# First maxima in four copies over four row groups, and a new order in the opening and the last steps

## The reference

```python
def _mlstm_head(q, k, v, ig, fg):              # per head, 8 heads of 64 channels
    log_fg = jax.nn.log_sigmoid(fg)
    cs = concatenate([0, cumsum(log_fg)])
    log_D = where(ltr, (cs - cs.T)[1:, 1:], -inf) + ig.T
    max_log_D = max(log_D, axis=-1)
    D = exp(log_D - max_log_D)
    C = (q @ (k.T / sqrt(DH))) * D
    normalizer = maximum(abs(C.sum(-1)), exp(-max_log_D))
    return C / (normalizer + EPS) @ v
...
def bitlinear(x, w):                            # x to 8 bit per token, w to -1, 0, 1 times mean(|w|)
    return act_quant(x) @ weight_quant(w).T
g = bitlinear(x, w_gate); u = bitlinear(x, w_up)
h = jnp.square(jax.nn.relu(g)) * u
return bitlinear(h, w_down)
...
x = x + tanh(g_xattn[0]) * attention(_layernorm(x), ctx, ctx, ...)   # heads then divided by their RMS
x = x + tanh(g_ffn[0]) * ffn(_layernorm(x), w_gate, w_up, w_down)
```

## Time and profile before

| | us |
|---|---|
| median of 3 runs | 612.44 |
| the profiled execution's own time | 614.58 |
| its span, first to last instruction | 612.9 |
| TensorE busy | 569.6 (93%) |
| VectorE busy | 526.9 (86%) |
| ScalarE busy | 452.7 (74%) |
| GpSimd busy | 125.9 (21%) |

### The profile page before, as it was taken

The page is one execution under the profiler, slowest core; times in us unless marked ns, Lnnn a source line. Parts: engine busy times, 40 slices in busy tenths (PEclk is TensorE's granted clock), DMA queues, the critical chain, the costliest instruction groups (busy, mean ns, idle before and its releaser), DMA issues.

```text
span 612.9 us, 18356 instructions
## 1 busy us (share of the span) xinstructions
PE 569.6 (93%) x6526; PEld 342.2 (56%) x6605; DVE 526.9 (86%) x1148; ACT 452.7 (74%) x923; POOL 125.9 (21%) x281
## 2 busy tenths in 40 slices
PE   7967578999999999999999999999999999999896
PEld 4744343656556565656556565656565565656443
DVE  4497989898989999898989899898989899897964
ACT  5578868868686868778687868778686968687662
POOL 2236151112121203012121212022121212021100
PEclk9589869999999999999999999999999999999999
DMA  8937305050230506050321405050412305030000
GB/s 319 383 132 250 130 2 190 3 182 28 94 115 18 189 0 206 0 189 17 134 72 39 167 17 189 0 194 13 164 42 76 130 18 190 2 105 1 22 33 34
DMA packets 44113, 62.68 MB, mean 102 GB/s; under 512 B 1848, under 2 KB 25648, under 8 KB 44080
## 3 DMA queue, kind: packets, MB, share of 16 engines
q1 hardware_dynamic: 44080, 62.24, 28.9%
HBM read 53.72 MB, written 8.51 MB: 102 GB/s over the span
## 4 chain that ended last, share of the span: by engine, by line
PE 80%; DVE 10%; issue 5%; ACT 2%; POOL 2%; DMA 1%; SPq 0%; DVEq 0%; ACTq 0%; POOLq 0%
PE yb L1181 17%; PE gb L1155 16%; PE ub L1155 16%; PE tp L1202 8%; PE ab L1189 7%; PE ab L1169 4%; PE tp L1229 3%; PE ab L1212 2%; PE ab L1190 2%; POOL stage L439 1%; PE ab L1263 1%; DVE asum L763 1%; DVE stage L785 1%; DVE dmat L898 1%; DVE stage L770 1%
## 5 line engine op out<-in xcount | busy, mean ns | idle before, releaser
L1155 PE MATMUL ub<-wuT,xqT 128*128 128x512 bf16 x498 | 129.4, 381 | 2.5 <-DVE stage L785 1.7
L1155 PE MATMUL gb<-wgT,xqT 128*128 128x512 bf16 x479 | 127.1, 382 | 4.9 <-issue 4.1
L1181 PE MATMUL yb<-wdT,stage 128*128 128x512 bf16 x482 | 114.3, 379 | 6.6 <-ACT stage L549 3.5
L535 ACT ACTIVATE relu<-gb 128x512 f32<-128x512 f32 x128 | 75.4, 589 | 48.8 <-PE gb L1155 48.4
L785 DVE TENSOR_TENSOR stage<-relu,ub 128x512 f32<-128x512 f32 x128 | 86.8, 678 | 15.9 <-ACT relu L537 15.9
L898 DVE SCALAR_TENSOR_TENSOR dmat<-ab,dmat 128x384 f32<-128x384 f32 x128 | 65.1, 549 | 25.8 <-POOL dmat L447 16.2
L1155 PEld LDWEIGHTS ub<-wuT,xqT 128*128 128x128 bf16 x512 | 49.6, 98 | 64.3 <-DVE stage L785 5.0
L537 ACT ACTIVATE relu<-relu 128x512 f32<-128x512 f32 x128 | 80.8, 631 | 4.1
L1181 PEld LDWEIGHTS yb<-wdT,stage 128*128 128x128 bf16 x512 | 47.0, 98 | 51.7 <-issue 4.3
L1155 PEld LDWEIGHTS gb<-wgT,xqT 128*128 128x128 bf16 x512 | 46.1, 101 | 45.4 <-issue 1.3
L447 POOL TENSOR_SCALAR_AFFINE_SELECT dmat<-dmat 128x256 f32<-128x256 f32 x128 | 55.6, 463 | 66.1 <-ACT dmat L595 50.6
(11 more groups left out here) (124 smaller groups left out, 886.6 us busy)
## 6 DMA issues: line engine op xcount, KB each, us to landing
dmat<-max_rows SPq DMA_DIRECT2D x15, 1024.0 KB, 5.0
values<-in_ctx_v SPq DMA_DIRECT2D x16, 520.0 KB, 7.6
xs<-in_x SPq DMA_DIRECT2D x16, 512.0 KB, 5.8
cT<-in_ctx_t SPq DMA_DIRECT2D x16, 512.0 KB, 6.8
out<-stage SPq DMA_DIRECT2D x32, 256.0 KB, 2.0
stage<-in_w_gate SPq DMA_DIRECT2D x4, 1024.0 KB, 12.2
stage<-in_w_up SPq DMA_DIRECT2D x4, 1024.0 KB, 13.1
stage<-in_w_down SPq DMA_DIRECT2D x4, 1024.0 KB, 5.4
```

The costliest lines, as they stand in the source:

```text
L535: nc.scalar.activation(relu[:, c % 2, :], gb[c % 2][:, :], ACT.Relu).then_inc(g_free, 1)
L1155: last = nc.tensor.matmul(bank[c % 2][:, :], xqT[par][:, t, d, :], w[:, d, c * CH:(c + 1) * CH], start=(d == 0), stop=(d == KD - 1))
L1181: done = nc.tensor.matmul(yb[:, :], hqT[:, c, :], wdT[:, c, :], start=(c == 0), stop=(c == KF - 1))
```

## The change

The scan of batch 0 runs on 128 partitions: a = ig - cs is written into four groups of 32 columns (8 used), so that its transpose has the 8 rows at partitions 0, 32, 64 and 96. `spread_first_max` then takes a different group of rows for each pair of heads. `pick` has ones in row (GROUP + 2) p + e of each group. The numbers of products of ones change, the total of the first weights comes after the next query transposes, and the total of the third weights after the gate products of step 0. Signs and roundings of weights are moved between engines and places. In the last two steps the copies and transposes of hidden values stand earlier.

```diff
-        pick = hq[0][0:NH, :].bitcast(F32)
+        pick = hq[0][:, 0:2 * 2 * P].bitcast(F32).rearrange("p (r c) -> p r c", r=2)
+        GROUP = P // NP
+        a_groups = sb("a_groups", [P, T, NP, GROUP], F32)
...
+            for g in range(NP):
+                if g > 0:
+                    gp.wait_ge(pick_step, g)
+                nc.gpsimd.affine_select(out=pick[:, :, :], in_=pick[:, :, :], compare_op=ALU.not_equal, fill=1.0,
+                                        base=-(GROUP + 2) * g, pattern=[[-1, 2], [0, P]], channel_multiplier=1).then_inc(pick_step, 1)
...  ScalarE, opening
             heads(0, 0)
-            exp_minus_max(0, 0)
             magnitudes(0, 2, 1)
-            for p in range(1, NP):
-                heads(0, p)
+            heads(0, 1)
+            exp_minus_max(0, 0)
+            heads(0, 2)
+            heads(0, 3)
...
-            sign_weight(0, 0)
             forget_gate(1)
             head_rms(0)
             magnitudes(1, 2, 3)
             magnitudes(1, 3, 4)
+            sign_weight(0, 0)
             tokens_rstd(0)
-            sign_weight(0, 1)
             sign_weight(1, 0)
             quantise_second(0)
             tokens(0, 0)
-            sign_weight(1, 1)
+            sign_weight(0, 1)
             exponentials(1, 0, 1)
...  ScalarE, step
+                if n is None:
+                    quantise_high(b - 1, 1)
                 relu_square(b, 0, 1)
...
-                if prev:
+                if n is None:
+                    hidden_cols(b - 1, 1)
+                elif prev:
                     quantise_high(b - 1, 1)
...
+                if m is None:
+                    hidden_cols(b, 0)
                 if n is not None:
                     tokens_rstd(n)
-                hidden_cols(b, 0)
+                if m is not None:
+                    hidden_cols(b, 0)
...  VectorE
+            def first_cumulative():
+                dve.wait_ge(tp_full, FULL * (gate_use(0, CUMSUM) + 1))
+                cs = tp[:, 0:T * NH].rearrange("p (t g) -> p t g", t=T)
+                nc.vector.tensor_tensor(a_groups[:, :, :, 0:NH], gates[:, :, None, 0:NH].to_broadcast([P, T, NP, NH]),
+                                        cs[:, :, None, :].to_broadcast([P, T, NP, NH]), ALU.subtract).then_inc(group_step, 1)
...
+            def first_running_max():
...
+                nc.vector.tensor_tensor_scan(mrows[:, :], tp[:, 0:S], zeros[:, :], LOWEST,
+                                             ALU.max, ALU.add).then_inc(tp_free, 1)
...
             scale_weight(1, 1)
+            round_weight(1)
...
                 hidden(b, 0, 2)
+                if n is None:
+                    hidden_cols(b - 1, 1)
...  TensorE
+            def spread_first_max():
...
                 for e in range(2):
-                    hd = 2 * p + e
-                    done = nc.tensor.matmul(spread_rows[p][:, e * S:(e + 1) * S], pick[:, hd * P:(hd + 1) * P], mrow[:, :],
-                                            start=True, stop=True)
-                done.then_inc(rows_spread, 1)
+                    for p in range(NP):
+                        rows = slice(GROUP * p, GROUP * p + NH)
+                        done = nc.tensor.matmul(spread_rows[p][:, e * S:(e + 1) * S], pick[rows, e, :], mrows[rows, :],
+                                                start=True, stop=True)
+                        if e == 1:
+                            done.then_inc(rows_spread, 1)
...
+            q_columns(1, 1)
+            keep_warm(2, yb)
             weight_total(0)
-            q_columns(1, 1)
             gate_products(1, 1, 0, T * 2 * KD)
             keep_warm(6, ub[1])
             cumulative_sum(1)
+            keep_warm(4, ub[1])
             a_rows(1, 1)
-            keep_warm(6, ub[1])
+            keep_warm(8, ub[1])
             weight_total(1)
             max_columns(1)
-            keep_warm(20, ub[1])
+            keep_warm(14, ub[1])
             token_columns(0)
...
+                if n is None:
+                    hidden_transposes(b - 1, 1)
                 chunk(b, 0, 3, par)
                 if n is not None:
                     heads_out(n, 2, npar)
-                if prev:
+                if prev and n is not None:
                     hidden_transposes(b - 1, 1)
-                else:
-                    weight_total(2)
...
+                if not prev:
+                    weight_total(2)
+                    chunk(b, 1, 0, par)
                     cumulative_sum(m)
+                    chunk(b, 1, 1, par)
+                    a_rows(m, par)
```

More of the change, by code:

```diff
@@ L186, in gated_block @@
         rows_spread = sem("rows_spread")
+        pick_step = sem("pick_step")
+        group_step = sem("group_step")
         max_stored = sem("max_stored")
@@ L1036, in step @@
                     weigh(n, 1)
+                hidden(b, 0, 0)
                 if not prev:
-                    scale_weight(1, 2)
                     round_weight(2)
-                hidden(b, 0, 0)
                 if m is not None:
@@ L1084, in step @@
                     log_forget(m)
+                if not prev:
+                    weight_scale(2)
+                    dve.wait_ge(winv_step, WINV[2])
+                    nc.vector.scalar_tensor_tensor(wprod[:, 2:3], wmean[:, 2:3], 1.0 / 127.0, tanhs[:, 1:2],
+                                                   ALU.mult, ALU.mult).then_inc(winv_step, 1)
                 if n is not None:
@@ L1264, in token_columns, with first_a_rows @@
                     last.then_inc(a_full[t], 1)
[L1266 to L1274 removed]
+            def first_a_rows():
+                pe.wait_ge(tp_free, gate_use(0, CUMSUM) + 1)
+                pe.wait_ge(group_step, 1)
+                for t in range(T):
+                    last = nc.tensor.transpose(tp[:, t * P:(t + 1) * P], a_groups[:, t, :, :].rearrange("p g w -> p (g w)"), ident[:, :])
+                last.then_inc(tp_full, FULL)
+            def spread_first_max():
+                pe.wait_ge(pick_step, NP)
+                pe.wait_ge(tp_free, gate_use(0, A_ROWS) + 1)
+                for e in range(2):
+                    for p in range(NP):
[4 more added lines that the diff above has]
+                            done.then_inc(rows_spread, 1)
             def keep_warm(count, bank):
@@ L1357, in step @@
                     down(b - 1, 1, KF // 2, KF)
-                if m is not None:
+                if not prev:
+                    weight_total(2)
+                    chunk(b, 1, 0, par)
                     cumulative_sum(m)
-                chunk(b, 1, 0, par)
-                if m is not None:
+                    chunk(b, 1, 1, par)
                     a_rows(m, par)
-                chunk(b, 1, 1, par)
+                else:
+                    if m is not None:
+                        cumulative_sum(m)
+                    chunk(b, 1, 0, par)
+                    if m is not None:
+                        a_rows(m, par)
+                    chunk(b, 1, 1, par)
                 hidden_transposes(b, 0)
```

59 lines of the change are left out of this document (26 added, 33 removed).

## The result

The changed kernel takes 625.21 us (median of 4 runs, 625.15 to 625.62) against 612.48 us (612.22 to 612.61) for the kernel before on the same chip: 1.021 times as long, interval 1.019 to 1.023. The forecast of 604.5 us, its range and the sign of all but one of its cases were wrong.

The account below looks back on a forecast made before the run. TensorE was taken to set the pace in the loop, dependencies and the clock in the opening. Terms -6.1, -0.7 and -0.3 gave -7.1, with -0.85 at the end -7.95: median 604.5 us, range 602 to 608.6.

Parts of the forecast that it names:

- the same 34.2 us a step: Loop: sign expected in the trace after the change, each step taking as long as before.
- row groups one after another: First maxima's two rounds: rival that row groups don't overlap, +1.4 us, 613.9; chance 6%.
- Constants and first maxima, +0.25: Opening: products start at 13.8 instead of 13.53, then two rounds of 0.6 us, done at 15.0; bounds 0 and 0.6.
- The clock stays full: Opening, first maxima onward: TensorE stays at 2.4 GHz; the rival that it falls anyway costs 2.6 us, 607.1, chance 20%.
- Head block, winv at 27.6: Opening, scores to first weights' rescaling: head groups end at 25.3 against 31.59, winv at 27.6 against 33.71; term -6.1 us.
- From winv to the first chunk, -0.7: Opening: gate's small work no longer queues behind ScalarE's rounding; chunk 0 starts near 45.5; -0.7 us.
- the rival of late weights: Opening: pieces land later than 2.7 us apiece, VectorE waits 2 to 4 us; 608 us; chance 6%.
- Third total, -0.3 left: Before step 1: TensorE's 3.25 us wait ahead of head group 3 goes, of which -0.3 us is left.
- GpSimd holds the step: End of step 0: GpSimd's pieces, factor and residual delay the statistics, -6.3 in place of -7.1 us; 605.9; chance 13%.
- Last steps, -0.85: Last two steps: earlier copies and transposes move ScalarE's activation from 597.42 to 596.6; -0.85 us, bounds 0 and -1.9.

Follow-up runs that it names:

- b_w30: Kernel before with 30 more instructions of already met semaphore waits ahead of the loop in TensorE's stream: 626.99 us, 1.025 times before.
- a_wide: Changed kernel with 14 of the first 16 and 13 of the last 14 products of ones replaced by three wide fp32 products each: 609.21 us, 0.9945 of before.
- a_warm1: Changed kernel with 1 product of ones at the very start in place of 16: 611.40 us.
- a_short: Changed kernel with a loop body 64 instructions shorter, some gate products of the first token tile left out (experiment only): 609.20 us.
- b_tail: Kernel before with the new order of the last two steps alone: 613.09 us, ratio 1.0007.
- b_spread: Kernel before with the first maxima alone in four copies and four row groups, 15 products of ones at the start: 610.43 us, 0.9947.
- b_w12: Kernel before with 12 more instructions of semaphore waits ahead of the loop: 612.40 us, one execution.
- b_w20: Kernel before with 20 more instructions of semaphore waits ahead of the loop: 622.55 us, one execution.
- a_wide_ws2: Changed kernel with wide fp32 products of ones at unchanged stream length, plus VectorE's winv of the third matrix moved back ahead of the hidden scale: 611.64 us.
- b_w120: Kernel before with 120 more instructions of semaphore waits ahead of the loop (also written +120): 652.93 us, one execution.
- a_w190: Changed kernel with 190 more instructions of already met waits ahead of the loop, between the first 16 products of ones: 625.63 us.

## Why the prediction was wrong

**The step that failed** is the first: "from 102.93 us to 547.22 us the loop runs at the full clock [...] whatever the opening gives back before 102.93 reaches the end unchanged", and with it "the same 34.2 us a step" in the list of signs. The change does not touch an instruction of the loop, so I gave the loop no term. It does move the loop in TensorE's stream: products of ones were counted as time (0.22 us each at full clock, those at the maxima hidden), and not as instructions. What took the term's place is +15.15 us, shown by `b_w30` (it appears without the change), by `a_wide` and `a_warm1` (it goes when the stream is as long as before) and by `a_short` (it goes when the body is shorter). None of the rivals was this one. The one slower case, row groups one after another, was the wrong mechanism.

The Trainium skill ("Runtime: NRT & Kernel Launch", Instruction fetch mechanics) says that a taken branch whose target lies outside the current window of two pages forces a fetch of the target's page before execution can go on, and that instructions come in blocks of 16 KiB or 256 instructions. Packet size and count here agree with the blocks (0.33 MB in 20), and the stall after the branch (5.6 us) agrees with the fetch. A window of two does not fit TensorE here: a body of 6.7 blocks runs from 168 to 500 us without a packet. The same section gives TensorE 128 KiB, which is eight blocks. By that a body that touches eight would be held whole, and at +120 (five misses in five) it is not. But every miss brings nine packets, one more than the body touches. If that one is the block behind the body, seven blocks and the one behind them fill the eight; whether it is so, no run shows.

**Constants and first maxima, +0.25.** The maxima started at 14.21, not 13.8: GpSimd's selects ended at 6.05 as said, but the first 16 products of ones took 6.4 us against 5.0, and the first gate products stood behind them (7.73 against 6.45). The two rounds took 1.14 us for eight products against 1.2 forecast, four side by side (four of the old ones, nearly all at full clock, take 2.0 in `b_tail`, so about 3.5 times as fast). Right, and the rival without overlap is gone.

**The clock stays full.** Right: 1.00 over 14 to 34 us. That the wider work ahead of the moment did it fits `b_spread`, which has fewer products of ones and falls near 17, but was not tried by itself. The products of ones ahead of scores 2 and 3 are seven more, not eight, since one stood there; they end at 18.26, and VectorE waits 0.67 us for the scores behind them, where I had nothing. What I did not follow is that the clock falls later, at 34 to 38 (0.57), 44 to 51 (0.54) and over most of 84 to 98 us (0.63). In the kernel before it is 1.00 over 34 to 38, and 0.94 over 88 to 102, the last 14 us ahead of its step 1. So the mean over the opening is 0.86 where it was 0.85.

**Head block, winv at 27.6.** Measured 27.58, where the earlier trace rows gives 33.71: the term of -6.1 holds against the profiled execution to 0.03 us, and so does its path: the last exponentials end at 20.44 (forecast 20.3), the last head group at 25.42 (25.3). Against the kernel's usual execution it does not. The old opening's clock came back at 28.1 in that execution, but within 26 to 28 us in `b_w12`, and the old opening's winv came at 31.68 to 34.11 and its first product of the loop at 100.76 to 103.18 in five executions (before, `b_tail`, `b_w12`, `b_w20`, `b_w30`). The one at 100.76 took 612.40 us, the usual time; the earlier trace rows show a late one. Loop and last steps take the same in both to 0.1 us, so the 2.1 us between profile and median lie ahead of step 1. I moved the sum over to the median unchanged, and so counted them as a gain. winv alone does not decide it: in `b_w30` it came at 31.68, and the first product of the loop at 103.18.

**From winv to the first chunk, -0.7.** The first chunk came 6.13 sooner, no more than winv. VectorE waited 0.62 us for the up-projection (the rival of late weights, at a tenth of its price), and the clock fell at 34.

**Third total, -0.3 left.** Mis-sized: measured +2.5 where I had -0.3 (99.33 - 102.93 = -3.6, after -6.1 at the first chunk). winv(2) stood ready at 78.31, not at 76.05, though its total was there at 73.97; GpSimd took 6.78, not 5.84, and the residual ended at 86.65 against 83.6 to 84.9 forecast. That is the rival "GpSimd holds the step", for which I had 0.8 us at step 1; here 2.8 are lost, which with the 0.7 of the term above are the 3.5 between 95.8 and 99.33. `a_wide_ws2` shows that GpSimd is a part of it only; the clock of 0.63 over 84 to 98 us, against 0.94 before, is another that the trace shows. How they share is not settled.

**Last steps, -0.85.** Measured -0.95 in the trace of after and -1.05 in `b_tail`.

Without the loop's term the forecast would still have been high: `a_wide`, which has the whole new order and no stall, takes 609.2, outside the range's upper end of 608.6 (which is itself 0.6 above the 608 of the weights' case that it names). Of the 4.7 us too much, 2.1 are the late execution taken for the usual one, and 2.4 the first product of the loop at 98.23 where I had 95.8.

## What to carry to other kernels

In a kernel with a loop, count the instructions that a change adds to each engine ahead of the loop, and read the instruction queue's packets: a loop that is fetched once has none while it runs, and when they appear, take some tens of instructions out ahead of the loop or out of its body. Here that brought 16 us (`a_wide`), while moving the loop to the next block with 190 idle instructions cost 14.7 us ahead of it and brought nothing in sum. A wait marked "issue" of several microseconds at the first product after the branch back was the sign of it. And before a sum is moved from the profiled execution to the median, find where the two differ, since that part can't be gained.

## What the runs showed of the hardware that I had not expected

- TensorE's loop of 1710 instructions is fetched once or again on the branch back depending on where it starts: 20 packets with 0 or 12 instructions more ahead of it, 29 to 65 with 20, 30 or 120 more, 21 with 220 more (the changed kernel with 190). Seven packets of 256 held and eight not fits all of them. A miss costs 3.6 to 5.6 us of standing still and half clock after it (in one of the nine in the traces, at 255.94 us in `b_w120`, the clock fell only behind the first products), 5 to 8 us in all, and nine packets.
- Near the edge only one or two of five branches back miss in the traces at +20, at +30 and of the changed kernel. The changed kernel's two misses are three iterations apart; in the old kernel with 30 waits the time scatters over 8.5 us from one execution to another. Why some are served is open.
- A straight stream of 52 packets has no stall and takes 1.6 us more over 445 us than the loop that is fetched once.
- The moment at which the clock comes back in the old opening differs by some 3 us between executions that have the same products (25 us in `b_w30`, 26 in `b_tail` and `b_w12`, 28 in `b_w20` and before), and the first product of the loop comes at 100.76 to 103.18.
- A wait already met is not free on TensorE: nearly 80 ns for an instruction of two, with the product behind it held up (`a_w190`).
